# A scan layer whose output product and bias run in fp32r passes, with rests taken by GpSimd

## The reference, cut to what matters

```
q, k = (x @ W_q.T), (x @ W_k.T)              # 8 heads of 64
v    = x @ W_v.T
b    = (q * k).sum(-1) / 8                   # one number per head and token
alpha = x @ W_alpha_w.T + W_alpha_b
a    = -softplus(alpha).sum(-1)              # one number per head and token
# state (ln, nm, sg) = log of the denominator, log and sign of the numerator
ln'  = logaddexp(a_t + ln, b_t)
ssum = sg * exp(a_t + nm - m) + sign(v_t) * exp(b_t + log(|v_t| + EPS) - m)
nm'  = m + log(|ssum| + EPS);  sg' = sign(ssum)
y_t  = sum over heads of sg' * exp(nm' - ln')
out  = y @ W_o.T
```

## Time and profile before

| | us |
|---|---|
| median of 3 runs | 2053.11 (2052.66 to 2054.73) |
| the profiled execution | 2054.83 |
| its span | 2053.0 |
| layer five up to step 0 | 1516.3 to 1553 |
| the 64 steps | 1553 to 1822 |
| from the last step to layer six | 1822 to 1831.2 |

### The profile page before, as it was taken

The page is one execution under the profiler, slowest core; times in us unless marked ns, Lnnn a source line. Parts: engine busy times, 40 slices in busy tenths (PEclk is TensorE's granted clock), DMA queues, the critical chain, the costliest instruction groups (busy, mean ns, idle before and its releaser), DMA issues. The chain is left out here.

```text
span 2053.0 us, 31444 instructions
## 1 busy us (share of the span) xinstructions
PE 1886.5 (92%) x10506; PEld 1503.4 (73%) x10506; DVE 1333.0 (65%) x2451; ACT 1125.2 (55%) x1864; POOL 136.0 (7%) x130
## 2 busy tenths in 40 slices
PE   7989985999997599999999999999968999889998
PEld 4657875999996578787878787878746767665664
DVE  4783547999995373636363636363538898877686
ACT  5762324888884353535454545454426676656663
POOL 0001000111110010000000000000000000002221
PEclk9999976999998799999999999999988988879999
DMA  6300042453524121101010101012031000020000
GB/s 234 107 31 1 2 167 82 162 195 125 193 72 174 62 83 42 36 31 39 27 50 17 51 15 51 15 51 81 17 119 63 1 1 1 1 88 0 1 21 21
DMA packets 22753, 129.81 MB, mean 63 GB/s; under 512 B 3602, under 2 KB 3858, under 8 KB 18963
## 3 DMA queue, kind: packets, MB, share of 16 engines
q1 hardware_dynamic: 17714, 112.59, 15.1%
q0 software_dynamic: 4960, 16.26, 2.4%
HBM read 116.51 MB, written 12.32 MB: 63 GB/s over the span
## 5 line engine op out<-in xcount | busy, mean ns | idle before, releaser
L116 PE MATMUL PS<-cT,qs 128*128 128x512 f32 x1152 | 300.3, 406 | 2.3 <-DVE qs L1682 2.2
L116 PE MATMUL PS<-pT,cN 128*128 128x512 f32 x1152 | 270.1, 392 | 1.7 <-DVE pT L1682 1.7
L116 PEld LDWEIGHTS PS<-cT,qs 128*128 128x128 f32 x1152 | 210.6, 189 | 52.3 <-issue 7.9
L116 PEld LDWEIGHTS PS<-pT,cN 128*128 128x128 f32 x1152 | 213.9, 188 | 45.4 <-DVE pT L1682 1.9
L116 PE MATMUL PS<-fw,xgT 128*128 128x384 f32 x1104 | 204.5, 340 | 5.7 <-DVE xgT L1224 5.7
L116 PEld LDWEIGHTS PS<-fw,xgT 128*128 128x128 f32 x1104 | 193.3, 190 | 9.2 <-DVE xgT L1224 6.3
L1677 DVE TENSOR_REDUCE nmax<-PS 128x1 f32<-128x512 f32 x128 | 87.6, 684 | 162.6 <-PE PS L116 162.5
L1224 DVE TENSOR_TENSOR fw<-W,fw 128x1536 fp32r<-128x1536 f32 x92 | 159.2, 1752 | 22.8 <-ACT fw L1147 22.8
L116 PE MATMUL PS<-xT,ws 128*128 128x512 f32 x576 | 155.1, 422 | 15.1 <-PEq L2575 8.7
L1582 ACT ACTIVATE qp<-PS 128x512 f32<-128x512 f32 x96 | 57.4, 598 | 189.6 <-PE PS L116 189.6
L1147 ACT ACTIVATE fw<-W 128x1536 fp32r x92 | 134.4, 1489 | 33.1 <-issue 33.1
(11 more groups left out here) (285 smaller groups left out, 3398.9 us busy)
## 6 DMA issues: line engine op xcount, KB each, us to landing
W<-in_fc SPq DMA_DIRECT2D x8, 3072.0 KB, 11.1
cT<-in_ctxT SPq DMA_DIRECT2D x16, 768.0 KB, 4.3
raw_pj<-in_proj SPq DMA_DIRECT2D x8, 1536.0 KB, 6.5
ct_in<-in_ctxT SPq DMA_DIRECT2D x16, 768.0 KB, 4.3
cn_in<-in_ctxN SPq DMA_DIRECT2D x16, 768.0 KB, 5.0
W<-in_w SPq DMA_DIRECT2D x2, 4096.0 KB, 13.7
routed_y<-y POOLq DMA_DIRECT2D x23, 256.0 KB, 2.3
W<-in_w SPq DMA_DIRECT2D x5, 1024.0 KB, 7.3
```

The source lines that it names most:

```text
L116: mm = nc.tensor.matmul(out, lhs(m, s), rhs(n, s), start=(opens and (s, m, n) == terms[0]), stop=((s, m, n) == terms[-1]))
```

## The change

- **Output product.** `wo` and y are kept in two fp32r parts; `out_proj` becomes `split_product`: 12 fp32r matmuls in the place of 4 fp32 ones. `wo` is split once, at c = 0, j = 5: first part on ACT (128 x 2048), rest on POOL (128 x 2048). y goes PSUM to `y_raw` (ACT `take_y`), to the first part (ACT `first_y`, at j = 3 of the next group), to the rest (POOL `rest_y`, 128 x 512). In the last group POOL's `rest_y` stands behind the root of seven columns.
- **Bias.** `bal` is split by one ACT copy (after one for a row of ones) and one DVE subtraction, right after the first weight; two fp32r matmuls replace the fp32 one.
- **Softplus in two pieces.** ln with its table load moves from `take_a` (j = 1) into `take_log`, behind the copy of q at j = 2. DVE's `softplus` moves from j = 2 behind `ep` to j = 3 between `s_` and `ep`; `products` moves to j = 3 behind `ep`.
- **In place.** `ear` writes into `ep`, `sg` into `ep`, the softplus into `lg`, q times k into `q`, and the sign term of v into `vt`. `s_`, `ep`, `bv`, `ebv` and others move into the large buffer `W0`.
- **DMAs.** The weights of the sixth layer are loaded after `wo` has been split, no longer before step 0.

The diff, cut to its core:

```diff
@@ sync
+                sp.wait_ge(w_lo, BASE + 1)
+                sp.dma_start(wo_in, a["w5"][:, W5_O]).then_inc(s_wo, 16)
                 sp.wait_ge(w_lo, BASE + 4)
+                sp.wait_ge(wo_lo, BASE + 1)
                 sp.dma_start(e.w16, a["w16"]).then_inc(e.s_w6, 16)
@@ gpsimd
+                def rest_y(c):
+                    pool.wait_ge(y_hi, BASE + c + 1)
+                    pool.wait_ge(z_mm, BASE + c)
+                    nc.gpsimd.tensor_tensor(yT[1][:, :, :].rearrange("p k t -> p (k t)"), y_raw,
+                                            yT[0][:, :, :].rearrange("p k t -> p (k t)").bitcast(F32),
+                                            ALU.subtract).then_inc(y_lo, 1)
+
+                ln.pool(pool, 0)
+                ln.pool(pool, 1)
                 for c in range(NG):
-                    ln.pool(pool, c)
+                    if c + 2 < NG:
+                        ln.pool(pool, c + 2)
+                    if c == 0:
+                        pool.wait_ge(wo_hi, BASE + 1)
+                        nc.gpsimd.tensor_tensor(wo[1][:, :, :], wo_in, wo[0][:, :, :].bitcast(F32),
+                                                ALU.subtract).then_inc(wo_lo, 1)
+                    else:
+                        rest_y(c - 1)
                 pool.wait_ge(var_sb, BASE + 1)
                 nc.gpsimd.tensor_tensor(e.rs6[:, 0:NT - 1], e.var6[:, 0:NT - 1],
                                         cn[:, CN_MHALF:CN_MHALF + 1].to_broadcast([P, NT - 1]), ALU.pow).then_inc(rs_sb, 1)
+                rest_y(NG - 1)
@@ tensor
-                        nc.tensor.matmul(bank, ones[0:1, :], bal[0:1, :], start=True, stop=False)
+                        for part in range(2):
+                            nc.tensor.matmul(bank, one[0:1, :], bals[part][0:1, :], start=(part == 0), stop=False)
...
-                    pe.wait_ge(yT_sb, BASE + 2 + c + 1)
+                    pe.wait_ge(y_lo, BASE + c + 1)
...
-                    for k in range(DK):
-                        mm = nc.tensor.matmul(ps[3], yT[:, c % 2, k, :], wo[:, k, :], start=(k == 0), stop=(k == DK - 1))
-                    mm.then_inc(z_mm, 1)
+                    split_product(nc, ps[3], lambda part, k: yT[part][:, k, :],
+                                  lambda part, k: wo[part][:, k, :], DK).then_inc(z_mm, 1)
@@ scalar
+                def take_log(c):
                     act.wait_ge(ex_sb, BASE + c + 1)
-                    act.wait_ge(a_used, BASE + c)
-                    nc.scalar.activation(lg, mag, ACT.Ln, bias=cn[:, CN_ONE:CN_ONE + 1]).then_inc(lg_sb, 1)
+                    nc.scalar.activation(lg, lg, ACT.Ln, bias=cn[:, CN_ONE:CN_ONE + 1]).then_inc(lg_sb, 1)
...
+                def first_y(c):
+                    act.wait_ge(yT_sb, BASE + 2 + c + 1)
+                    act.wait_ge(z_mm, BASE + c)
+                    nc.scalar.activation(yT[0][:, :, :].rearrange("p k t -> p (k t)"), y_raw, ACT.Copy).then_inc(y_hi, 1)
...
                 first_w(0)
+                act.wait_ge(s_bal, BASE + 16)
+                nc.scalar.activation(one[:, :], ones[0:1, :], ACT.Copy)
+                nc.scalar.activation(bals[0][:, :], bal, ACT.Copy).then_inc(bal_hi, 1)
                 first_w(1)
...
                         elif j == 2 and c + 1 < NG:
                             take_q(c + 1)
-                        elif j == 3 and c + 1 < NG:
-                            first_v(c + 1)
+                            take_log(c + 1)
+                        elif j == 3:
+                            if c + 1 < NG:
+                                first_v(c + 1)
+                            if c >= 1:
+                                first_y(c - 1)
+                        elif j == 5 and c == 0:
+                            act.wait_ge(s_wo, BASE + 16)
+                            nc.scalar.activation(wo[0][:, :, :], wo_in, ACT.Copy).then_inc(wo_hi, 1)
...
                 take_y(NG - 1)
+                first_y(NG - 1)
@@ vector
                 rest_w(0)
+                ve.wait_ge(bal_hi, BASE + 1)
+                nc.vector.tensor_tensor(bals[1][:, :], bal, bals[0][:, :].bitcast(F32), ALU.subtract).then_inc(bal_lo, 1)
                 rest_w(1)
...
                         elif j == 3 and c + 1 < NG:
-                            products(c + 1)
+                            softplus(c + 1)
...
-                        elif j == 2 and c + 1 < NG:
-                            softplus(c + 1)
+                        elif j == 3 and c + 1 < NG:
+                            products(c + 1)
```

More of the change, by code:

```diff
@@ L1794, in decayed_attention_layer @@
         ws = [sbuf(f"ws5{part}", [P, 4, DK, D], F32R) for part in range(2)]
-        mag, lg, soft, q, qk, vt = (W0[:, 8192 + n * D:8192 + (n + 1) * D] for n in range(6))
+        lg, q, vt, v0, s_, ep = (W0[:, 8192 + n * D:8192 + (n + 1) * D] for n in range(6))
         pick_in = W0[:, 11264:11264 + G * P]
-        wo = W0[:, 12288:12288 + DK * D].rearrange("p (k n) -> p k n", k=DK)
+        y_raw = W0[:, 11264:11264 + D]
+        bv, ebv = (W0[:, 12288 + n * 2 * D:12288 + (n + 1) * 2 * D].rearrange("p (n d) -> p n d", n=2) for n in range(2))
+        bal = W0[0:1, 14336 - D:14336]
+        wo_in = W0[:, 0:DK * D].rearrange("p (k n) -> p k n", k=DK)
+        wo = [sbuf(f"wo5{part}", [P, DK, D], F32R) for part in range(2)]
         rb = W0[:, 14336:14336 + RB * D].rearrange("p (n d) -> p n d", n=RB)
@@ L1802, in decayed_attention_layer @@
         vs = [sbuf(f"vs5{part}", [P, 2, D], F32R) for part in range(2)]
-        bal = sbuf("bal5", [1, D])
+        bals = [sbuf(f"bals5{part}", [1, D], F32R) for part in range(2)]
+        one = sbuf("one5", [1, P], F32R)
         xT = [[sbuf(f"xT5{u}{part}", [P, DK, P], F32R) for part in range(2)] for u in range(2)]
-        v0, veps = sbuf("v05", [P, D]), sbuf("veps5", [P, D])
         ba, spread, own = sbuf("ba5", [P, 2 * HS]), sbuf("spread5", [P, G, 2 * HS]), sbuf("own5", [P, 2 * G, HS])
@@ L1810, in decayed_attention_layer @@
                                                                        "eal5", "ebe5"))
-        bv, ebv = sbuf("bv5", [P, 2, D]), sbuf("ebv5", [P, 2, D])
-        ear, s_, ep, sg = (sbuf(n, [P, D]) for n in ("ear5", "s5", "ep5", "sg5"))
-        yT = sbuf("yT5", [P, 2, DK, P])
+        yT = [sbuf(f"yT5{part}", [P, DK, P], F32R) for part in range(2)]
         ln = Norm(nc, e, "5", sbuf, ps[3], xT[0])
         s_x5 = [sem(f"s_x5_{c}") for c in range(NG)]
+        bal_hi, bal_lo, wo_hi, wo_lo = sem("bal_hi5"), sem("bal_lo5"), sem("wo_hi5"), sem("wo_lo5")
+        y_hi, y_lo = sem("y_hi5"), sem("y_lo5")
         s_wk, s_wo, s_bal, s_pick = sem("s_wk5"), sem("s_wo5"), sem("s_bal5"), sem("s_pick5")
@@ L1839, in _ @@
                 sp.dma_start(w_in[:, 3], a["w5"][:, W5_K]).then_inc(s_wk, 16)
-                sp.dma_start(bal[:, :], a["ba5"]).then_inc(s_bal, 16)
+                sp.dma_start(bal, a["ba5"]).then_inc(s_bal, 16)
                 sp.wait_ge(e.s_xd, BASE + 16 * NT)
@@ L1930, in _ @@
                 pe.sem_inc(y_mm, RB)
-                pe.wait_ge(s_bal, BASE + 16)
+                pe.wait_ge(bal_lo, BASE + 1)
                 turn_x(0)
@@ L1941, in _ @@
                     values(t)
-                pe.wait_ge(s_wo, BASE + 16)
                 for c in range(NG):
@@ L1980, in take_v @@
                     act.wait_ge(vt_sb, BASE + c)
-                    nc.scalar.activation(v0[:, :], ps[0], ACT.Copy).then_inc(v_sb, 1)
+                    nc.scalar.activation(v0, ps[0], ACT.Copy).then_inc(v_sb, 1)
                 def first_v(c):
@@ L2022, in _ @@
                 take_a(0)
+                take_log(0)
                 take_q(0)
@@ L2038, in scaled @@
                                          scale=ebe[:, t:t + 1]).then_inc(ebv_sb, 1)
+                act.wait_ge(bal_lo, BASE + 1)
                 scaled(0)
@@ L2046, in _ @@
                             act.sem_inc(seen)
-                            nc.scalar.activation(ear[:, cols], rb[:, (t - 1) % RB, cols], ACT.Abs,
+                            nc.scalar.activation(ep[:, cols], rb[:, (t - 1) % RB, cols], ACT.Abs,
                                                  scale=eal[:, t:t + 1]).then_inc(ear_sb, 1)
@@ L2201, in _ @@
                             ve.wait_ge(ear_sb, BASE + 2 * t + h + 1)
-                            nc.vector.tensor_tensor(ep[:, cols], ear[:, cols], ebv[:, t % 2, cols],
+                            nc.vector.tensor_tensor(ep[:, cols], ep[:, cols], ebv[:, t % 2, cols],
                                                     ALU.max).then_inc(ep_sb, 1)
@@ L2223, in _ @@
                             ve.wait_ge(sg_sb, BASE + 2 * t + h + 1)
-                            nc.vector.tensor_tensor(new[:, cols], s_[:, cols], sg[:, cols], ALU.add).then_inc(r_sb, 1)
+                            nc.vector.tensor_tensor(new[:, cols], s_[:, cols], ep[:, cols], ALU.add).then_inc(r_sb, 1)
                 ve.wait_ge(z_used, BASE + NG - 1)
```

30 lines of the change are left out of this document (15 added, 15 removed).

## The result

The changed kernel takes 2061.64 us (median of 7 runs, 2059.61 to 2065.43), the kernel before beside it 2053.11 (2051.46 to 2055.52): 1.0039 times as long, with a 95% interval of 1.0029 to 1.0049. It is slower by 8.5 us; the forecast was 16.2. The profiled execution took 2065.43 (span 2063.6), the slowest of its seven; a second profiled one (span 2058.5) gives the spread.

| stretch | before | after | after, second time |
|---|---|---|---|
| ahead of layer five (to the last addition of layer four, L1718) | 1512.7 | 1516.0 | 1511.4 |
| from there to the `s_` of step 0 | 40.6 | 41.8 | 41.5 |
| the 64 steps, to the last half of the last r | 268.1 | 266.8 | 266.6 |
| from there to the last addition (L2155, after L2197) | 7.8 | 13.8 | 13.8 |
| the rest | 223.9 | 225.2 | 225.2 |

A forecast was written before the change was run, and what follows sets the result against it. DVE was taken to set the length of the steps, PE mattering only where it makes ACT late. The terms 3.2 - 5.0 + 7.3 + 4.8 + 5.9 gave +16.2 us on 2053.11, so 2069, in a range of 2056 to 2080.

The forecast's parts named there:

- Part 1: In the 64 steps, softplus split and shorter PE products cut DVE's waits: -5.0 us (ends +1 and -10).
- Part 2: POOL's rests stall DVE in the steps: +7.3 us for seven `rest_y`, +4.8 for the rest of `wo`.
- Part 3: At the start, ACT waits for `bal` behind the K weights, delaying statistics, weights and step 0: +3.2 us.
- part 4: At the end, the last `rest_y` queues behind POOL's root and delays the last output product: +5.9 us.
- the count from `ear`: Timing ACT and DVE from step 2's `ear` start gave a new softplus wait of 0.9 to 1.3 us per group.
- in the late groups the q product is the next thing late: In late groups q comes 4.2 us behind the alpha product, ln follows it, so the split itself gains nothing.
- Part "nothing": In-place results, the later load of the sixth layer's weights and other POOL roots were put at no cost.
- the second rule: A drain of about 1.38 us per ACT table switch would lengthen step 3's wait in seven groups: +9.7, 2079 us.
- POOL stalls nothing: Rival: POOL's rests don't stall DVE, as its operands lie elsewhere: +4.1, 2057 us; chance 0.10.
- The lower clock for longer: Rival: PE idles more at steps 3 to 5, so products run at the low clock: +13, 2082 us; chance 0.12.
- The passes bring nothing: Rival: the output product's twelve passes take as long as the eight records, 2 us less gain: 2071 us; chance 0.08.
- Faster: Rival: DVE's waits in the steps go wholly and POOL stalls nothing: -9.6, 2043 us; chance 0.05.

The follow-up runs named there:

- a_memset: The changed kernel with POOL writing zeros where it subtracted, so the rests of y and `wo` are left out; 2051.40 us.
- b_split: The kernel before plus only the softplus in two pieces, output product and bias still fp32; 2049.81 us.
- b_bias: The kernel before plus only the bias in two fp32r passes; 2049.23 us.
- best1: The changed kernel with `bal` loaded first, last `rest_y` ahead of the root, `wo` split before step 0, `first_y` at step 1, `rest_y` held for DVE's wait; 2048.30 us.
- a_tail: The changed kernel with the last `rest_y` ahead of the root in POOL's queue; 2058.03 us.
- a_bal: The changed kernel with the DMA of `bal` issued ahead of the K weights; 2060.73 us.
- b_ kernel: Any kernel made of the kernel before plus a part of the change: softplus split 2049.81 us, bias passes 2049.23, both 2048.90.

## Why the prediction was right and wrong

**The sign and the range held.** The forecast was slower, 2069 in 2056 to 2080; it is 2061.6. Of the 16.2 us forecast 8.5 came, half of it. The range held by its width: parts 1 to 3 all came out lower than forecast, part 4 was right, and the 1.3 us in the sixth layer had been put at nothing.

**Part 1, forecast -5.0, measured -10.9: the step that failed.** The new wait at step 3 was foreseen as 0.9 to 1.3 us in each of seven groups. It is 0.59, 1.52, 0.81, 0.82, 0.81, 0.81 and 1.26 in the groups 0 to 6, so the count from `ear` was near. What PE gives back was near for the output product (forecast 4.4 us, measured 4.05 to 4.50).

Wrong was the step "in the late groups the q product is the next thing late", which priced the split there at nothing and let 4.2 us behind a late alpha product stay. It took for granted that the alpha product stays as late in groups 4 to 6. But in groups 4 and 6, as in group 1, its lateness was that of the long record of the product itself, 4.61 instead of 3.07. None is long in either execution of the changed kernel, and q was late for ACT in groups 1 and 6 alone, by 0.82 and 0.33 us. (Why it is never long there stays open: `a_memset`, with the same passes, has two.) Where a long product stays, the step holds: in `b_split` groups 1, 3 and 6 have one, and ACT waits 0.94 us for q in each; groups 4 and 5 have none, and 0.81 and 0.91 us of waits stand there where before had 2.8 and 2.3. The row was in the trace of before and the prediction read only the product of group 3, a short one. `b_bias` shows what makes the difference, -6.9 in the steps for an edit priced at 0.6 a group. Its own size, 0.39 and not 0.6 for the bias, was the smaller error, and the terms as listed add up to -5.2, not -5.0.

**Part 2, forecast +12.1, measured +9.7: right in its mechanism, mis-sized.** `rest_y` costs 0.73 six times (forecast 1.05), as POOL starts 0.4 us ahead of the spreading, under the reduction, and 1.05 once in group 7; `wo` costs 4.30 (forecast 4.8). `a_memset` and `best1` together show that it takes POOL's reading and two SBUF inputs on DVE. The row that the price came from has its 1.1 us beside a POOL instruction of 1.60, not 1.29. The Trainium skill (SBUF — State Buffer, Who interferes with whom) has the two exclude each other for the whole instruction: 4.30 of 4.59 us bears it out, and the fixed price of 1.1 that the row alone would have allowed is refuted.

**Part 3, forecast +3.2, measured +0.9 to 1.3.** `bal` came with the K weights as said (ACT waited 2.82 us), and the first statistics began 14.6 us behind L1718 where 12.2 had stood: 2.4 of the 3.6. Half of this was taken up before step 0, where DVE's wait for `bv` shrank from 2.7 to 1.2 us. The prediction passed the delay through a stretch that had that much idle time in it.

**Part 4, forecast +5.9, measured +6.0.** Each step of it is in the rows above; `a_tail` takes 4.5 of them back by the queue's order alone.

**Part "nothing" and the second rule.** In-place results cost nothing that can be seen: with the stalls away (`a_memset`) the steps are 259.4 us, shorter than in any b_ kernel. ACT, group 2 of after, in order of time:

```profile
1641.66 1.28 ACT L2019 ACT_TABLE_LOAD   x1
1642.96 0.72 ACT L2019 ACTIVATE W<-W,cn 128x512 f32<-128x512 f32 x1
1643.59 0.90 ACT L2081 ACTIVATE W<-W,eal 128x256 f32<-128x256 f32 x2
```

ln starts 0.02 us behind the load, and the load 0.02 us behind the copy of q, so the drain that the Trainium skill adds (ScalarE: Activation LUTs, What ACT_TABLE_LOAD costs) isn't there, and 2079 fell with it.

**The rivals.** "POOL stalls nothing" is out by the 5.05 us row. The lower clock for longer is out for the steps: no alpha product is long. "The passes bring nothing" is out, since the output product took 4.05 to 4.50 us where the prediction read 5.07. "Faster" failed on the stalls, but its first half, waits that go nearly wholly, came closer to the truth than the forecast. Its bound ("9.1 us of waits and stalls") was passed by far: 7.8 + 9.7 = 17.5.

## What to carry to other kernels

Before work goes to GpSimd because it is idle, look at what VectorE does beside it: where VectorE's instruction reads two SBUF tiles and GpSimd reads SBUF too, VectorE can stand still for nearly all of GpSimd's instruction, and doing the work there can be cheaper; put it where VectorE waits or reads at most one SBUF tile. Read the duration of the same product in every group, not in a quiet one, since three long records of seven can carry half of an engine's waits. And of a change with several parts try each alone: here the bias saved 7 us in the steps, and the output product as built cost 13.

## What the runs showed of the hardware

- A POOL subtraction of 128 x 2048 (4.59 us) held one DVE operation with two SBUF inputs for 4.30 us; a POOL memset of the same size (1.80 us, `a_memset`) held none; DVE instructions with one PSUM and one SBUF input, and reductions of one SBUF input, ran at full speed beside POOL's subtraction. Between DVE's back-to-back instructions with two SBUF inputs POOL was held too: 3.07 for 1.29 (`best1`, group 7).
- POOL takes 1.26 us for 512 columns and 4.59 for 2048: about 1.1 for each 512 and 0.15 fixed, so the large one is only 9% cheaper by the column.
- A bias row in two fp32r passes takes 0.73 us against 1.12 in fp32, and the alpha product behind it ran into the low clock in 8 of 77 cases instead of 7 of 21. The link is a count, not a cause.
- A DMA of 2 KB issued behind 1024 KB on the same queue kept ACT waiting for 2.82 us; issued ahead (`a_bal`), it kept nobody waiting.
- The sixth layer, the same code in all kernels, took 221.8 us where its first 10 us had a granted clock of 0.83 (before) and 223.1 where it was 0.66 (the changed kernel, twice).
